# The last feed-forward of a two-layer block on one core: first-half products made and stored beside the second half's routing

## The chip, the core and the metric

One core of one Trainium2 chip runs the whole program as a single launch. The metric is the device time in microseconds; three runs of the kernel before gave a median of 1976.43 us (1968.13 to 1978.0). The core has TensorE (PE; its weight loads are PEld), VectorE (DVE), ScalarE (ACT), GpSimd (POOL) and SyncE (SP). ACT and SP can each issue DMAs on a queue of their own; both queues are served by the same 16 DMA engines.

## The reference

The input is 16 sequences of 256 tokens of 256 numbers. Two attention layers and two feed-forward layers are applied with residual sums. The change touches only the last feed-forward:

```
grouped = x.reshape(b, s // 32, 32, d)                       # 128 groups n of 32 tokens t
logits  = einsum('bntd,des->bntes', grouped, Wc) + bc + tie  # 32 x 4 = 128 experts (e, s)
perm    = (logits == max over t of logits)                   # each expert takes one token of each group
permuted = einsum('bntd,bntes->bnesd', grouped, perm)
inner   = relu(einsum('bnesd,esdf->bnesf', permuted, W1) + b1)   # 256 -> 32
result_permuted = einsum('bnesf,esdf->bnesd', inner, W2) + b2    # 32 -> 256
result  = einsum('bnesd,bntes->bntd', result_permuted, perm)
```

So result_permuted holds 128 groups x 128 experts x 256 float32 numbers, 16 MB, and it does not fit on the core beside the rest. The kernel writes it to HBM (`rp_scratch`, called `rpd`, laid out group, expert, number) and reads it back in another order.

## The kernel before

All five engines run a hand-written program whose order is fixed by semaphores. The last feed-forward begins in the last slots of the attention loop and has two parts.

**Routing, in 20 steps** (`pe_step`, `dve_step`, `act_step`, `pool_step`, n = 0 to 19). A batch b holds 256 tokens, 8 groups. In step n, PE transposes the choice of batch n-2 (L1511), computes the logits of batch n-1 (L1519), transposes the tokens of batch n (L1527) and gathers the chosen tokens of batch n-3 (L1545) into four PSUM banks called `GATHER` (3, 4, 5, 7). ACT copies three of these banks and DVE the fourth into the tile `PX` (L1720, L1633). `PX` has room for 64 groups, so it is filled twice: "halves" 0 and 1. The gather of the next batch waits until these copies are done, since it uses the same four banks. In step 11 (`UP_AT`) PE multiplies half 0 with all of W1 (`pe_up`, L1571, four calls of 32 experts, each with its own 1-MB load of W1), and DVE writes the result with bias and relu into `INT` (`dve_up`). Then routing goes on for batches 9 to 15, into the same `PX`.

**The tail.** `pe_up` for half 1, then 16 calls of `down(q2)`: the second product of 8 experts for all 128 groups, 8 matmuls with 128 groups as output rows into one set of four PSUM banks; DVE and ACT copy two banks each into a 1-MB buffer `RP` (L1703, L1732), and SP stores it (L1779): 128 rows of 8 KB, one per group. The number of `RP` buffers is two for the first four calls and four after them. When all 16 stores have landed, SP reads the 16 MB back (L1787), 8 groups at a time, with experts as partitions, in 1-KB pieces, into six buffers `R2`; PE applies the transpose of the choice (`back`, L1605 and L1608), DVE adds the residual (L1710) and ACT issues the output (L1736), 256 KB for each batch.

SP issues all loads of W1 and W2: six loads of W1 (`first`, L1757) as their buffers come free, two of W2 (`second`, L1761) when the last gather is done, two of W1, then two more of W2 among the stores. In total W1 is read twice (8 MB) and W2 once (4 MB).

The store before is one line. Its destination has 128 rows outermost, as has its source:

```
e.dma_start(rpd[:, 8 * q2:8 * q2 + 8, :], RP[out_at(q2)][:, :, :, :].rearrange("p q r d -> p (q r) d"))
```

Of the kernel before, what the change touches and what calls it, by code (L numbers as in the profile page):

```python
# [56 lines left out]
def build(nc, A, OUT):  # L57
# [1121 lines left out]
    d_ys = [sem(f"d_ys{i}") for i in range(2)]  # L1179
# [109 lines left out]
    def dve_ffn(e, w):  # L1289
# [120 lines left out]
    d_vl = [sem(f"d_vl{i}") for i in range(2)]  # L1410
# [46 lines left out]
    WF2P = [Arena(nc, x3_at)("WF2P0", [128, 8, 256], fp32)]  # L1457
# [3 lines left out]
    WF2P.append(Arena(nc, q1_at)("WF2P1", [128, 8, 256], fp32))  # L1461
    WF1P = [mem_t(f"WF1P{i}", [128, 2, 32, 32], fp32) for i in range(2)]
# [12 lines left out]
    R2 = [mem_t(f"R2{i}", [128, 8, 256], fp32) for i in range(NR)]  # L1475
# [3 lines left out]
    wt_sent, kl_sent = 16, 16 * 32  # L1479
    d_r2 = [sem(f"d_r2{i}") for i in range(NR)]  # L1480
# [10 lines left out]
    def down_set(q2):  # L1491
        return q2 % 2 if q2 >= 4 else 0

    def out_at(q2):
        return q2 % 2 if q2 < 4 else 2 + q2 % 4

    def out_of(q2):

        return q2 - 2 if q2 in (2, 3) else q2 - 4 if q2 >= 8 else None

    def taken_of(q2):

        return q2 if q2 <= 4 else q2 - 1

    def pe_step(e, w, n):
# [25 lines left out]
        def gather(b):  # L1531
# [4 lines left out]
            w.wait_ge(s_in, 7 if b == 8 else 0)  # L1536
            w.wait_ge(a1.s_tv, 2 * U)
# [20 lines left out]
        if n == UP_AT:  # L1558
            for j in range(4):
                pe_up(e, w, 0, j)  # L1560
        if is_batch(n - 3):
            gather(n - 3)

    def pe_up(e, w, hf, j):
        w.wait_ge(d_kl_wf1[j % 2], kl_sent + 16 * (2 * hf + j // 2 + 1))
        w.wait_ge(s_px, 24 * (hf + 1))
        w.wait_ge(s_py, 8 * (hf + 1))
        for q in range(8):
            for cc in range(2):
# [4 lines left out]

    def pe_tail(e, w):
        def down(q2):
            w.wait_ge(d_wt_wf2[q2 // 4 % 2], wt_sent + 16 * (q2 // 8 + 1))
            w.wait_ge(s_in, 8 + 2 * (q2 // 4) + 2)
            w.wait_ge(s_rb, 32)
            w.wait_ge(s_x3e, 16)  # L1580
            w.wait_ge(s_pm, 48)
            w.wait_ge(s_pb, 16)
            w.wait_ge(s_e0, taken_of(q2))
            w.wait_ge(s_e1, taken_of(q2))
            w.wait_ge(s_in, 16 if q2 >= 4 else 0)
            for q in (2 * q2, 2 * q2 + 1):
                for r in range(4):
                    rows = slice(32 * r, 32 * r + 32)
                    m = e.matmul(PS[DOWN[down_set(q2)][r]][:, q % 2 * 256:q % 2 * 256 + 256], INT[rows, q, :],
                                 WF2P[q // 8 % 2][rows, q % 8, :], start=True, stop=True)  # L1590
            m.then_inc(s_fm, 1)

# [96 lines left out]
    def rp_free(w, q2):  # L1689
        if q2 >= 4:  # L1690
            w.wait_ge(s_u3, 8)
        p = out_of(q2)
        if p is not None:
            w.wait_ge(d_ks_rp[p % 4], ks_sent + 16 * (p // 4 + 1))

    def dve_tail(e, w):
        dve_up(e, w, 1, 0)
        dve_up(e, w, 1, 1)
        for q2 in range(16):
            w.wait_ge(s_fm, q2 + 1)  # L1700
            rp_free(w, q2)
            for r in range(2):
# [606 lines left out]
```

## Time and profile before

| | |
|---|---|
| median of 3 runs | 1976.43 us |
| the profiled execution: its own time | 1972.35 us |
| its span, first to last instruction | 1970.5 us |
| PE, DVE, ACT, POOL busy | 90%, 72%, 57%, 39% |
| mean granted TensorE clock | 0.957 |
| last feed-forward, from the first `pe_up` to the end (1799.6 to 1970.5 us) | 170.9 us |

The page gives averages of the whole span; in its 40 slices the last seven (each 49.3 us) differ from the rest. Views used: the stretches ("windows": busy time of each engine, granted clock, DMA busy share of the 16 DMA engines, GB/s), the chain of work that ended last, the instructions in order of time, the DMA view (packets, sizes, issue to landing), and the rows of single source lines.

### The profile page before, as it was taken

The page shows a single profiled execution, that of the slowest core. Times are in us where ns is not written, and L with a number is a line of the kernel's source. Part 1 is how long each engine was busy: PE and PEld are TensorE (multiplying, and loading weights), DVE is VectorE, ACT ScalarE, POOL GpSimd, SP SyncE. Part 2 cuts the span into 40 slices and gives each one's busy share as a digit, 9 for nine tenths or more (in the row PEclk, how much of TensorE's full clock was granted, in tenths as well). Part 3 has the DMA queues.
Part 4 walks back from the last instruction along what each step waited for, and adds up shares of the span by engine and source line. Part 5 has one row for each costly group of instructions (what it writes and reads, how often), then busy time and mean ns, then how long its engine had stood idle before and what let it go on. Part 6 is the DMA issues. An engine that isn't in the chain of part 4 may idle for free.

```text
span 1970.5 us, 41315 instructions
## 1 busy us (share of the span) xinstructions
PE 1774.4 (90%) x15920; PEld 1480.3 (75%) x15920; DVE 1416.2 (72%) x2887; ACT 1129.7 (57%) x2812; POOL 776.3 (39%) x1160
## 2 busy tenths in 40 slices
PE   4788889889899999999999978999999999997647
PEld 3565656656889899999999967887888888876522
DVE  4667777774271488888898658999999999766521
ACT  1344555553334677777777557777777777743310
POOL 1202221101001133333333168788888887644100
PEclk8789999999999999999999989999999999999867
DMA  6444433332577666666776752222222221112599
GB/s 195 108 76 87 86 81 82 80 85 92 202 280 252 226 231 246 247 239 234 248 248 222 245 180 65 65 86 66 66 87 66 65 87 55 53 47 88 202 368 328
DMA packets 134116, 298.70 MB, mean 152 GB/s; under 512 B 13152, under 2 KB 77408, under 8 KB 118688
## 3 DMA queue, kind: packets, MB, share of 16 engines
q1 hardware_dynamic: 111520, 186.18, 30.5%
q0 software_dynamic: 18048, 105.69, 15.6%
q10 hardware_dynamic: 4352, 4.20, 0.6%
q8 instruction: 126, 2.06, 0.4%
q14 instruction: 70, 0.57, 0.1%
HBM read 207.93 MB, written 87.82 MB: 150 GB/s over the span
## 4 chain that ended last, share of the span: by engine, by line
PE 72%; DVE 13%; DMA 7%; issue 3%; POOL 2%; ACT 2%; SPq 1%; DVEq 0%; POOLq 0%; ACTq 0%
PE ps L1232 11%; PE ps L1218 11%; PE ps L1814 5%; PE ps L362 5%; PE ps L214 4%; PE ps L1845 4%; PE ps L1834 4%; PE ps L1800 4%; PE ps L368 3%; PE ps L464 2%; DVE NM L601 2%; DMA R<-rp_scratch 2%; DVE NM L180 2%; PE ps L453 2%; PE ps L441 2%
## 5 line engine op out<-in xcount | busy, mean ns | idle before, releaser
L191 ACT ACTIVATE P<-ps,NM 128x256 f32<-128x256 f32 x512 | 235.8, 474 | 157.3 <-DVE NM L180 157.2
L204 POOL TENSOR_TENSOR P<-P,RS 128x1024 f32<-128x1024 f32 x128 | 246.0, 1922 | 84.9 <-DVE RS L198 84.5
L601 DVE TENSOR_REDUCE NM<-ps 128x2 f32<-128x512 f32 x256 | 164.7, 686 | 111.7 <-PE ps L441 111.6
L1218 PE MATMUL ps<-XRP,W1P 128*128 128x256 f32 x1872 | 226.5, 281 | 4.1 <-DVE W1P L1301 4.1
L712 ACT ACTIVATE PT<-ps 128x512 f32<-128x512 f32 x256 | 138.7, 593 | 150.1 <-PE ps L453 147.9
L1218 PEld LDWEIGHTS ps<-XRP,W1P 128*128 128x128 f32 x1872 | 219.8, 190 | 4.4 <-DVE W1P L1301 4.4
L1232 PE MATMUL ps<-W2P,HP 128*128 128x256 f32 x1872 | 221.3, 277 | 0.0
L1232 PEld LDWEIGHTS ps<-W2P,HP 128*128 128x128 f32 x1872 | 217.7, 188 | 0.0
L138 POOL TENSOR_TENSOR LTMP<-RSTD 128x2 f32<-128x2 f32 (+1 forms) x156 | 32.3, 207 | 351.1 <-DVE RSTD L131 342.8
L180 DVE TENSOR_REDUCE NM<-ps 128x2 f32<-128x512 f32 x256 | 164.2, 683 | 4.9 <-PE ps L1800 3.0
L1261 ACT ACTIVATE HF<-ps,WE 128x256 f32<-128x256 f32 x312 | 129.0, 465 | 43.8 <-PE ps L1218 43.8
L1152 POOL DMA_INDIRECT WE<-in_we,WIX x39 | 44.4, 1139 | 276.2 <-DVE W1P L1301 209.9
L1800 PEld LDWEIGHTS ps<-K,Q 64*128 64x128 f32 x1536 | 101.7, 190 | 59.8 <-issue 47.0
L221 ACT ACTIVATE PT<-ps 128x512 f32<-128x512 f32 x256 | 140.3, 614 | 1.2 <-PE ps L214 1.2
L1814 PE MATMUL ps<-PT,V 128*64 128x256 f32 x1024 | 138.8, 392 | 1.6 <-DVE OT L1935 1.6
L1800 PE MATMUL ps<-K,Q 64*128 64x256 f32 x1536 | 128.3, 300 | 11.0 <-DVE Q L1927 6.2
L214 PE MATMUL ps<-CST,P 128*128 128x128 f32 x1024 | 133.5, 273 | 1.9 <-ACT PT L221 1.5
L1252 ACT ACTIVATE W2P<-WE 128x512 fp32r<-128x512 f32 x156 | 97.3, 623 | 53.1 <-PE ps L1232 53.1
L1148 POOL DMA_INDIRECT XR<-xn_scratch,RIX x78 | 79.0, 1012 | 107.8 <-PE ps L1194 51.0
L1834 PE MATMUL ps<-XNP,W1Q 128*128 128x256 f32 x768 | 111.6, 296 | 9.3 <-POOL XNP L2107 9.3
L214 PEld LDWEIGHTS ps<-CST,P 128*128 128x128 f32 x1024 | 115.1, 141 | 3.4 <-issue 2.5
L1318 DVE TENSOR_TENSOR HP<-HF,HP 128x512 fp32r<-128x512 f32 x156 | 108.0, 693 | 13.0 <-ACT HP L1268 4.0
(220 smaller groups left out, 3832.4 us busy)
## 6 DMA issues: line engine op xcount, KB each, us to landing
KS<-k_scratch SPq DMA_DIRECT2D x64, 256.0 KB, 3.5
V<-v_scratch SPq DMA_DIRECT2D x16, 1024.0 KB
rp_scratch<-RP SPq DMA_DIRECT2D x16, 1024.0 KB
R<-rp_scratch SPq DMA_DIRECT2D x16, 1024.0 KB, 14.0
k_scratch<-KVM SPq DMA_DIRECT2D x54, 256.0 KB
QS<-q_scratch SPq DMA_DIRECT2D x96, 128.0 KB, 4.3
v_scratch<-KVM SPq DMA_DIRECT2D x40, 256.0 KB
ys_scratch<-YS SPq DMA_DIRECT2D x39, 256.0 KB, 8.3
```

What stands on the lines that cost most here:

```text
L180: e.tensor_reduce(self.NM[:, u % 4, 2 * x:2 * x + 2], PS[SB[n % 3]][:, :].rearrange("p (h j) -> p h j", h=2), AX.X, ALU.max, negate=True). ...
L191: i = e.activation(self.P[u % 4][:, c, :], PS[SB[n % 3]][:, y * 256:y * 256 + 256], ACT.Exp, bias=self.NM[:, u % 4, c:c + 1], accum_out=se ...
L204: e.tensor_tensor(p, p, self.RS[:, u % 4, :].unsqueeze(2).to_broadcast([128, 4, 256]), ALU.mult).then_inc(self.s_pn, 1)
L214: i = e.transpose(PS[TB[h]][:, c0:c0 + 128], self.P[u % 4][:, c, jt * 128:jt * 128 + 128], ident)
L221: e.activation(self.PT[u % 4][h][:, :], PS[TB[h]][:, :], ACT.Copy).then_inc(self.s_tv, 1)
L601: e.tensor_reduce(NM0[b % 2][:, :, 8 * h + p], PS[SB[(2 * u + h) % 3]][:, :].rearrange("p (l j) -> p l j", l=2), AX.X, ALU.max, negate=Tru ...
L712: e.activation(PT0[u % 4][h][:, :], PS[TB[h]][:, :], ACT.Exp).then_inc(s_ex0, 1)
L1218: m = e.matmul(PS[p][:, hh * 256:hh * 256 + 256], W1P[i % 2][wi][:, cc * 1024 + hc * 128:cc * 1024 + hc * 128 + 128], XRP[i % 2][xi][:, cc ...
L1232: m = e.matmul(PS[4 + k][:, s * 256:s * 256 + 256], HP[k][hi][:, hc, s * 128:s * 128 + 128], W2P[k][wi][:, hc * 256:hc * 256 + 256], start ...
L1800: m = e.matmul(PS[SB[(2 * u + h) % 3]][:, lt * 256:lt * 256 + 256], Q1[i][64 * h:64 * h + 64, p, lt * 128:lt * 128 + 128], K1[j][64 * h:64 ...
L1814: m = e.matmul(PS[OB][64 * h:64 * h + 64, 0:256], V1[b % 2][:, jt, (2 * p + h) * 64:(2 * p + h) * 64 + 64], a1.PT[u % 4][h][:, jt * 256:jt ...
L1834: m = e.matmul(QB[:, j * 256:j * 256 + 256], W1Q[wi][:, cc, c0:c0 + 128], XNP[b % 2][xi][:, cc, :], start=(cc == 0 and x == 0), stop=(cc = ...
```

## The change

- The second products of half 0 are made in steps 12 to 19, one call of `pe_down(n)` per step ahead of the gather, instead of in the tail. Each call now makes the products of 16 experts for the 64 groups of one half: 16 matmuls of 64 output rows. Experts q with j = 0 go to PSUM rows 0 to 63 and those with j = 1 to rows 64 to 127. There are again 16 calls, 8 for each half, and each fills a 1-MB buffer.
- Calls 0 to 5 use the four `GATHER` banks, since the other banks hold the routing. `pe_down(n)` waits until the last gather was copied out, and the next gather waits until ACT and DVE have copied the products (`s_e0`, `s_e1`). Calls 6 to 9 use the other set.
- The buffer's partition is (j, group), and SP's store has the destination pattern "j p (x d)": 2, then 64 groups, then 8 KB. The source stays 128 partitions of 8 KB. Ten calls use two `RP` buffers; then there are four.
- W2 is read for each half; its last quarter is kept from the first to the second half, so 7 MB instead of 4. The loads of W1 for half 1 all come after step 18. The late loads (four of W1, three of W2) are issued by ACT, the early ones by SP.
- ACT issues the first two of the 16 reads of `rpd` after call 11 (their eight groups each belong to half 0), and SP issues reads 2 to 5 as each of the last four stores has landed. The rest come when all have.
- Some semaphores are used for a second purpose (`d_ys_rp`, `d_vl_rp`); this adds no instruction.

```diff
-    WF2P = [Arena(nc, x3_at)("WF2P0", [128, 8, 256], fp32)]
+    WUP = {"C": Arena(nc, x3_at)("WUPC", [128, 2, 32, 32], fp32)}
+    WDN = {"C": Arena(nc, x3_at)("WDNC", [128, 8, 256], fp32)}
...
-    WF2P.append(Arena(nc, q1_at)("WF2P1", [128, 8, 256], fp32))
-    WF1P = [mem_t(f"WF1P{i}", [128, 2, 32, 32], fp32) for i in range(2)]
+    WDN["D"] = Arena(nc, q1_at)("WDND", [128, 8, 256], fp32)
+    for x in "AB":
+        WDN[x] = Arena(nc, mem_t.at)(f"WDN{x}", [128, 8, 256], fp32)
+        WUP[x] = mem_t(f"WUP{x}", [128, 2, 32, 32], fp32)
...
-    R2 = [mem_t(f"R2{i}", [128, 8, 256], fp32) for i in range(NR)]
+    R2 = [mem_t(f"R2{i}", [128, 8, 256], fp32) for i in (2, 3, 4, 5, 0, 1)]
+    R2 = R2[4:] + R2[:4]
...
+    LATE_STORES = ((d_ys_rp[0], 16 * 20), (d_ys_rp[1], 16 * 19), (d_vl_rp[0], 16 * 8), (d_vl_rp[1], 16 * 8))
...
-    def down_set(q2):
-        return q2 % 2 if q2 >= 4 else 0
-    def out_at(q2):
-        return q2 % 2 if q2 < 4 else 2 + q2 % 4
-    def out_of(q2):
-        return q2 - 2 if q2 in (2, 3) else q2 - 4 if q2 >= 8 else None
-    def taken_of(q2):
-        return q2 if q2 <= 4 else q2 - 1
+    LOADS = {"A": (d_kl_wf1[0], kl_sent), "B": (d_kl_wf1[1], kl_sent), "C": (d_wt_wf2[0], wt_sent), "D": (d_wt_wf2[1], wt_sent)}
+    UP_IN = (("A", 1), ("B", 1), ("A", 2), ("B", 2), ("A", 5), ("C", 1), ("A", 6), ("C", 2))
+    DOWN_IN = (("A", 3), ("B", 3), ("A", 4), ("B", 4), ("D", 1), ("A", 7), ("C", 3), ("B", 4))
+    def loaded(w, at):
+        d, n0 = LOADS[at[0]]
+        w.wait_ge(d, n0 + 16 * at[1])
+    def down_set(n):
+        return 1 if n < 6 else 0 if n < 10 else n % 2
+    def out_at(n):
+        return n % 2 if n < 10 else 2 + n % 4
+    def out_of(n):
+        return n - 2 if 2 <= n < 10 else n - 4 if n >= 14 else None
+    def taken_of(n):
+        return 0 if n == 6 else n if n <= 10 else n - 1
...
+            w.wait_ge(s_e0, min(b - 8, 6))
+            w.wait_ge(s_e1, min(b - 8, 6))
...
+        if n > UP_AT:
+            pe_down(e, w, n - UP_AT - 1)
         if is_batch(n - 3):
             gather(n - 3)
+    def pe_down(e, w, n):
+        at = DOWN_IN[n // 2]
+        hf, t = n // 8, n % 8
+        loaded(w, at)
+        w.wait_ge(s_in, 8 * hf + 2 * (t // 2) + 2)
+        if n < 6:
+            w.wait_ge(s_px, 3 * (n + 9))
+            w.wait_ge(s_py, n + 9)
+        else:
+            w.wait_ge(s_rb, 32)
+            w.wait_ge(s_x3e, 16)
+            w.wait_ge(s_pm, 48)
+            w.wait_ge(s_pb, 16)
+        w.wait_ge(s_e0, taken_of(n))
+        w.wait_ge(s_e1, taken_of(n))
+        w.wait_ge(s_in, 16 if n >= 10 else 0)
+        for k in range(2):
+            for j in range(2):
+                q = 4 * t + 2 * j + k
+                for r in range(4):
+                    rows = slice(32 * r, 32 * r + 32)
+                    m = e.matmul(PS[DOWN[down_set(n)][r]][64 * j:64 * j + 64, k * 256:k * 256 + 256],
+                                 INT[rows, q, hf * 64:hf * 64 + 64], WDN[at[0]][rows, q % 8, :], start=True, stop=True)
+        m.then_inc(s_fm, 1)
...
-        for q2 in range(16):
-            down(q2)
-            if q2 < 2:
-                pe_up(e, w, 1, q2 + 2)
+        for n in range(8, 16):
+            pe_down(e, w, n)
+            if n < 10:
+                pe_up(e, w, 1, n - 6)
...
+        if n > UP_AT:
+            dve_out(e, w, n - UP_AT - 1)
...
+    def landed(w, n):
+        if n < 8:
+            w.wait_ge(d_ks_rp[n % 4], ks_sent + 16 * (n // 4 + 1))
+        else:
+            d, n0 = LATE_STORES[n % 4]
+            w.wait_ge(d, n0 + 16 * (n // 4 - 1))
...
+    def rp_free(w, n):
+        w.wait_ge(s_om, 32)
+        w.wait_ge(s_u3, 8 if n >= 10 else 0)
+        p = out_of(n)
         if p is not None:
-            w.wait_ge(d_ks_rp[p % 4], ks_sent + 16 * (p // 4 + 1))
+            landed(w, p)
...
+    def dve_out(e, w, n):
+        w.wait_ge(s_fm, n + 1)
+        rp_free(w, n)
+        for r in range(2):
+            i = e.tensor_copy(RP[out_at(n)][:, :, r, :], product(n, r))
+        i.then_inc(s_e0, 1)
+    def act_out(e, w, n):
+        w.wait_ge(s_fm, n + 1)
+        rp_free(w, n)
+        for r in range(2, 4):
+            i = e.activation(RP[out_at(n)][:, :, r, :], product(n, r), ACT.Copy)
+        i.then_inc(s_e1, 1)
...
+        if n > UP_AT:
+            act_out(e, w, n - UP_AT - 1)
+        if n == UP_AT + 7:
+            w.wait_ge(s_fm, 6)
+            first(e, 4)
+            w.wait_ge(s_x3p, 32)
+            w.wait_ge(s_x3t, 16)
+            first(e, 5)
+        elif n == UP_AT + 8:
+            w.wait_ge(s_ga, 16)
+            second(e, 4)
     def act_tail(e, w):
-        w.wait_ge(s_om, 32)
-        for q2 in range(16):
-            w.wait_ge(s_fm, q2 + 1)
-            rp_free(w, q2)
-            for r in range(2, 4):
-                i = e.activation(RP[out_at(q2)][:, :, r, :], PS[DOWN[down_set(q2)][r]][:, :].rearrange("p (q d) -> p q d", q=2), ACT.Copy)
-            i.then_inc(s_e1, 1)
+        for j in (6, 7):
+            w.wait_ge(s_u3, j - 1)
+            first(e, j)
+        act_out(e, w, 8)
+        w.wait_ge(s_u3, 7)
+        second(e, 5)
+        act_out(e, w, 9)
+        w.wait_ge(s_u3, 8)
+        second(e, 6)
+        act_out(e, w, 10)
+        act_out(e, w, 11)
+        for n in range(4):
+            landed(w, n + 4)
+        for b in range(2):
+            back_in(e, w, b)
+        for n in range(12, 16):
+            act_out(e, w, n)
...
+    def first(e, j):
+        x = UP_IN[j][0]
+        e.dma_start(WUP[x][:, :, :, :], A["wf1"][:, :, 32 * (j % 4):32 * (j % 4) + 32, :]).then_inc(LOADS[x][0], 16)
+    def second(e, j):
+        x = DOWN_IN[j][0]
+        e.dma_start(WDN[x][:, :, :], A["wf2"][:, 8 * (j % 4):8 * (j % 4) + 8, :]).then_inc(LOADS[x][0], 16)
+    def back_in(e, w, b):
+        w.wait_ge(s_cm2, b - NR + 1)
+        e.dma_start(R2[b % NR][:, :, :], rpd[8 * b:8 * b + 8, :, :].rearrange("n s d -> s n d")).then_inc(d_r2[b % NR], 16)
     def sp_tail(e, w):
-        def first(j):
-            w.wait_ge(s_u3, j - 1)
-            e.dma_start(WF1P[j % 2][:, :, :, :], A["wf1"][:, :, 32 * (j % 4):32 * (j % 4) + 32, :]).then_inc(d_kl_wf1[j % 2], 16)
-        def second(j):
-            w.wait_ge(s_fm, 4 * (j - 1))
-            e.dma_start(WF2P[j % 2][:, :, :], A["wf2"][:, 8 * j:8 * j + 8, :]).then_inc(d_wt_wf2[j % 2], 16)
+        def store(n):
+            hf, t = n // 8, n % 8
+            w.wait_ge(s_e0, n + 1)
+            w.wait_ge(s_e1, n + 1)
+            to = rpd[64 * hf:64 * hf + 64, 16 * t:16 * t + 16, :].rearrange("p (j x) d -> j p (x d)", j=2)
+            e.dma_start(to, RP[out_at(n)][:, :, :, :].rearrange("p k r d -> p (k r d)")).then_inc(LATE_STORES[n % 4][0] if hf else d_ks_rp[n % 4], 16)
...
-        for j in range(6):
-            first(j)
-        w.wait_ge(s_ga, 16)
-        second(0)
-        second(1)
-        first(6)
-        first(7)
-        for q2 in range(16):
-            w.wait_ge(s_e0, q2 + 1)
-            w.wait_ge(s_e1, q2 + 1)
-            e.dma_start(rpd[:, 8 * q2:8 * q2 + 8, :], RP[out_at(q2)][:, :, :, :].rearrange("p q r d -> p (q r) d")).then_inc(d_ks_rp[q2 % 4], 16)
-            if q2 in (3, 7):
-                second(q2 // 4 + 2)
         for j in range(4):
-            w.wait_ge(d_ks_rp[j], ks_sent + 16 * 4)
-        w.wait_ge(s_u3, 8)
-        for b in range(16):
-            w.wait_ge(s_cm2, b - NR + 1)
-            e.dma_start(R2[b % NR][:, :, :], rpd[8 * b:8 * b + 8, :, :].rearrange("n s d -> s n d")).then_inc(d_r2[b % NR], 16)
+            w.wait_ge(s_u3, j - 1)
+            first(e, j)
+        for j in range(2):
+            w.wait_ge(s_u3, j + 3)
+            second(e, j)
+        for n in range(8):
+            store(n)
+            if n in (1, 3):
+                w.wait_ge(s_fm, n + 1)
+                second(e, n // 2 + 2)
+        for n in range(8, 16):
+            store(n)
+        for b in range(2, 6):
+            landed(w, 10 + b)
+            back_in(e, w, b)
...
+        for n in range(8, 12):
+            landed(w, n + 4)
+        for b in range(6, 16):
+            back_in(e, w, b)
```

## Rows read from the trace of the kernel before

**Rows 1.** The page: engines, and DMA in 40 slices of 49.3 us.

```profile
PE 1774.4 (90%) x15920; PEld 1480.3 (75%) x15920; DVE 1416.2 (72%) x2887; ACT 1129.7 (57%) x2812; POOL 776.3 (39%) x1160
...
DMA  6444433332577666666776752222222221112599
GB/s 195 108 76 87 86 81 82 80 85 92 202 280 252 226 231 246 247 239 234 248 248 222 245 180 65 65 86 66 66 87 66 65 87 55 53 47 88 202 368 328
```

**Rows 2.** Stretches: step 11, steps 12 to 19, products and stores, last landing, reads.

```profile
core 0: us, PE busy (x) PEld busy (x) DVE busy (x) ACT busy (x) POOL busy (x), PEclk, DMA share, GB/s
...
1799.60:1815.00 15.40, 9.53 (x516) 8.78 (x516) 5.73 (x13) 0.58 (x1) 0.53 (x1) 0.89 0.53 178
1815.00:1840.40 25.40, 18.16 (x305) 15.13 (x307) 16.03 (x36) 15.27 (x28) 11.59 (x12) 0.90 0.20 67
1840.40:1897.30 56.90, 34.19 (x768) 25.98 (x768) 24.87 (x40) 17.32 (x32) 0.00 (x0) 0.77 0.91 361
1897.30:1905.80 8.50, 0.00 (x0) 0.00 (x0) 0.00 (x0) 0.00 (x0) 0.00 (x0) 0.50 0.70 297
1905.80:1970.50 64.70, 44.09 (x320) 18.38 (x320) 11.00 (x16) 0.00 (x0) 0.00 (x0) 0.73 0.96 325
```

**Rows 3.** The chain of work that ended last, 1838 to 1912 us: start, length, what.

```profile
1871.94 11.24 DMA rp_scratch<-RP
...
1884.59 11.25 DMA rp_scratch<-RP
...
1895.94 1.30 DVE RP L1703 x2
1897.24 0.02 issue
1897.26 8.40 DMA rp_scratch<-RP
```

**Rows 4.** Stretches of saturated stores, and of saturated reads with output.

```profile
1870.00:1900.00 30.00, 12.69 (x136) 8.07 (x128) 12.23 (x20) 10.23 (x20) 0.00 (x0) 0.72 1.01 421
1912.00:1960.00 48.00, 36.72 (x271) 15.35 (x272) 8.93 (x13) 0.00 (x0) 0.00 (x0) 0.75 1.09 368
```

**Rows 5.** In order of time, a routing step: start, length, instruction, [idle before].

```profile
1814.95 1.11 PE L1545 MATMUL ps<-PB,X3P 32*128 32x128 f32 x32 [0.88 <-DVE RL L1684]
...
1818.70 0.66 PE L1527 MATMUL ps<-CST,X 128*128 128x128 f32 x4 [1.40 <-issue]
...
1819.29 1.11 PE L1545 MATMUL ps<-PB,X3P 32*128 32x128 f32 x32
...
1820.46 1.63 ACT L1720 ACTIVATE PX<-ps 128x512 f32<-128x512 f32 x3 [0.46 <-PE ps L1545]
...
1822.19 1.07 PE L1545 MATMUL ps<-PB,X3P 32*128 32x128 f32 x29
```

**Rows 6.** In order of time, one call of down and its copies.

```profile
1848.07 1.15 PE L1589 MATMUL ps<-WF2P,INT 32*128 32x256 f32 x16
...
1849.29 1.29 DVE L1703 COPY RP<-ps 128x512 f32<-128x512 f32 x2
1849.35 1.09 ACT L1732 ACTIVATE RP<-ps 128x512 f32<-128x512 f32 x2 [9.05 <-PE ps L1589]
```

**Rows 7.** DMA view, 68.9 to 71.5 us: four 4-KB transfers of eight 512-byte pieces.

```profile
DMA packets 64, 0.02 MB, mean 6 GB/s; under 512 B 32, under 2 KB 64, under 8 KB 64
```

**Rows 8.** DMA view, 1734 to 1741 us: one transfer of 128 rows of 1 KB, then others.

```profile
DMA packets 156, 0.18 MB, mean 26 GB/s; under 512 B 16, under 2 KB 144, under 8 KB 156
...
B<-in_b SPq DMA_DIRECT2D x1, 128.0 KB, 2.0
```

**Rows 9.** DMA view, 1870 to 1900 us: packets of the saturated stores.

```profile
DMA packets 1729, 12.62 MB, mean 421 GB/s; under 512 B 191, under 2 KB 191, under 8 KB 191
```

**Rows 10.** SP's queue in order of time: issues.

```profile
1838.71 0.81 SPq L1761 DMA_DIRECT2D WF2P<-in_wf  x2
1844.09 4.63 SPq L1757 DMA_DIRECT2D WF1P<-in_wf  x2
...
1877.29 20.28 SPq L1779 DMA_DIRECT2D rp_scratch<-RP  x8
1905.80 8.87 SPq L1787 DMA_DIRECT2D R<-rp_scratch  x5
```

**Rows 11.** Stretches around a fall of the granted clock in the routing.

```profile
1776.00:1788.00 12.00, 7.21 (x119) 5.93 (x118) 11.52 (x34) 5.68 (x11) 8.02 (x25) 0.99 0.01 2
1788.00:1791.00 3.00, 3.00 (x14) 2.20 (x13) 2.07 (x6) 1.07 (x2) 2.52 (x6) 0.50 0.00 0
1819.30:1833.70 14.40, 12.17 (x199) 10.10 (x199) 11.46 (x27) 10.49 (x19) 9.34 (x10) 1.00 0.02 5
```

More of the change, by code:

```diff
@@ L1178, in build @@
     assert mem.at <= base1 + FFN_AT
-    d_ys = [sem(f"d_ys{i}") for i in range(2)]
+    d_ys_rp = [sem(f"d_ys_rp{i}") for i in range(2)]
     s_ft, s_xrp, s_um, s_ge, s_hp = sem("xrT"), sem("xrp"), sem("upmm"), sem("gelu"), sem("hp")
@@ L1409, in build @@
     d_gy = [sem(f"d_gy{i}") for i in range(4)]
-    d_vl = [sem(f"d_vl{i}") for i in range(2)]
+    d_vl_rp = [sem(f"d_vl_rp{i}") for i in range(2)]
     s_ca, s_wh, s_wl, s_tanh = sem("moe_add"), sem("wqo_hi"), sem("wqo_lo"), sem("tanh")
@@ L1575, in pe_tail @@
     def pe_tail(e, w):
[L1576 to L1591, printed above, removed]
         def back(b):
@@ L1698, in dve_tail @@
         dve_up(e, w, 1, 1)
-        for q2 in range(16):
-            w.wait_ge(s_fm, q2 + 1)
-            rp_free(w, q2)
-            for r in range(2):
-                i = e.tensor_copy(RP[out_at(q2)][:, :, r, :], PS[DOWN[down_set(q2)][r]][:, :].rearrange("p (q d) -> p q d", q=2))
-            i.then_inc(s_e0, 1)
-            if q2 < 2:
-                dve_up(e, w, 1, q2 + 2)
+        for n in range(8, 16):
+            dve_out(e, w, n)
+            if n < 10:
+                dve_up(e, w, 1, n - 6)
         for b in range(16):
@@ L1768, in sp_tail @@
         e.dma_start(B2[:, :], A["b2_1"]).then_inc(d_c1, 16)
-        for j in range(6):
-            first(j)
-        w.wait_ge(s_ga, 16)
-        second(0)
-        second(1)
-        first(6)
-        first(7)
-        for q2 in range(16):
-            w.wait_ge(s_e0, q2 + 1)
-            w.wait_ge(s_e1, q2 + 1)
-            e.dma_start(rpd[:, 8 * q2:8 * q2 + 8, :], RP[out_at(q2)][:, :, :, :].rearrange("p q r d -> p (q r) d")).then_inc(d_ks_rp[q2 % 4], 16)
-            if q2 in (3, 7):
-                second(q2 // 4 + 2)
-        for j in range(4):
-            w.wait_ge(d_ks_rp[j], ks_sent + 16 * 4)
-        w.wait_ge(s_u3, 8)
-        for b in range(16):
-            w.wait_ge(s_cm2, b - NR + 1)
-            e.dma_start(R2[b % NR][:, :, :], rpd[8 * b:8 * b + 8, :, :].rearrange("n s d -> s n d")).then_inc(d_r2[b % NR], 16)
+        for j in range(4):
+            w.wait_ge(s_u3, j - 1)
[8 more added lines that the diff above has]
+                second(e, n // 2 + 2)
+        for n in range(8, 16):
+            store(n)
[6 more added lines that the diff above has]
+            back_in(e, w, b)
         for j in range(4):
@@ L2060, in act_l1 @@
             late_out(e, w, t)
-        w.wait_ge(d_ys[0], 16 * 20)
-        w.wait_ge(d_ys[1], 16 * 19)
+        w.wait_ge(d_ys_rp[0], 16 * 20)
+        w.wait_ge(d_ys_rp[1], 16 * 19)
         w.wait_ge(s_ye, NTF)
@@ L2109, in pool_l1 @@
         w.wait_ge(s_ft, NTF)
-        w.wait_ge(d_ys[0], 16 * 20)
-        w.wait_ge(d_ys[1], 16 * 19)
+        w.wait_ge(d_ys_rp[0], 16 * 20)
+        w.wait_ge(d_ys_rp[1], 16 * 19)
         for j in range(4):
```

20 lines of the change are left out of this document (9 added, 11 removed).

## The prediction, made before the changed kernel was seen to run

> **What bounds the kernel now.** I read the page first. PE is busy for 90% of the span, but the DMA rows show that the last slices are another kind of work: 202 to 368 GB/s, against 47 to 88 before them [rows 1]. The stretches of the last feed-forward then show who works [rows 2]. While half 1 is routed (1815 to 1840 us) the DMA engines are at 0.20 of their time and PE at 18.2 of 25.4 us. After 1840.4 it is the reverse: DMA share 0.91, then 0.70, then 0.96. The chain of waits says the same: from 1871.9 us it consists of stores to `rp_scratch`, 11.2 us at a time, with a 1.3-us copy between them, until the last store has landed (8.4 us after the last copy) [rows 3]. In saturated stretches the 16 engines move 421 GB/s of stores and 368 GB/s of reads with outputs, both at a share of 1.01 or more [rows 4]. So the tail is bound by the DMA engines, and PE's granted clock there (0.72 to 0.77) costs little. The idea of the change follows from these rows: 8 MB of stores, 20 us at 421 GB/s, move into a stretch in which DMA idles. What it is worth hangs on whether a store in its new form still runs at 421 GB/s.
>
> **Part 1: the routing steps become longer.** A step is now 2.90 us: gather (started 1819.29), copy to `PX` by ACT (1820.46, 1.63 us), next gather at 1822.19 [rows 5]. In steps 12 to 17 a call and its copies come in between, since they use the gather's banks: 1.22 us from the call to DVE's copy (1848.07 to 1849.29), 1.29 us of copy, and 0.2 us until the waiting PE goes on [rows 6]. That is 2.7 us on the path, six times: 16 us. ACT's two copies (1.09 us) lie beside DVE's. The call has 16 matmuls of 64 output rows where the row has 8 of 128; if these overlap as before it stays 1.15 us, and if not at all it is 2.3 us, 7 us more in six steps. I take 1.15, because the work per bank is the same. A longer step leaves PE emptier, and before the clock's fall to 1.2 GHz (share 0.50) at 1788 us PE was busy for 60% of 12 us, against 85% in the steps of now at full clock [rows 11]. A step would have about 4.1 of 5.6 us, 73%, so a fall or two of 3 us is to be expected: 1 to 5 us. Behind the waiting PE are queued only the next gather, behind ACT's wait its copies and loads.
>
> **Part 2: the loads.** W1's four loads of half 1 come after call 5's products are copied, where two of them had been there early and two were issued at 1844 to 1848 us [rows 10]; W2 is read in 7 pieces instead of 4. At 421 GB/s [rows 4] a 1-MB load holds all engines for 2.5 us. ACT issues seven of them, at some 0.5 us each, ahead of copies that aren't urgent then.
>
> **Part 3: the form of the stores.** This decides. Before, both sides of a store have 128 rows outermost. Now the destination has 2, then 64, then 8 KB. What number of engines does a transfer use? The DMA view shows it. Four transfers of eight 512-byte pieces have 32 data packets and 32 packets below 512 bytes [rows 7], 8 small ones for each transfer. A transfer of 128 rows of 1 KB has 128 data packets and 16 small ones [rows 8]. The small packets are no data (the pieces alone make up the 4 KB), so I read them as one signal of each engine that took part: 8 engines where the outermost count is 8, 16 where it is 128. If the outermost count sets it, a new store runs on 2 engines, one for each j. All rows of before fit this reading, but none has a small outermost count with many rows inside, so it isn't proved by them.
>
> The Trainium skill states that case: "DMA: Bandwidth & Descriptors", section "Why a DMA increments its semaphore by 16 and not by 1", says that the transfer is split along the slowest dimension other than 1 of each side, over the largest number of engines up to 16 that divides both. The trace agrees for 8 and for 128; by it the store here would run on 2. It adds that these are always the lowest-numbered ones; no row shows it.
>
> The price: 421 GB/s over 16 engines is 26.3 GB/s for each [rows 4], and the stores' packets are 8 KB there already (1538 of 1729 packets are not under 8 KB; the others are below 512 bytes) [rows 9], so an engine can't gain from larger ones. 1 MB over two engines takes 1048576 / 52600 = 19.9 us instead of 2.5. All 16 stores come from one queue. If each takes the same pair, these two engines are one lane through which everything passes, the loads' and reads' sixteenth parts too.
>
> **The sum of the forecast.** Call 0 starts where gather 9 did, at 1819.3; with 1.2 and 1.3 us [rows 6] its store is issued at 1821.9 and flows from some 1823.0. Then the pair has to do: 16 stores of 19.9 = 318.4 us; nine 1-MB loads (two early ones of W2 behind stores in SP's queue, seven late ones) of 2.5 = 22.5; the two reads ahead of the rest, 1 MB at 368 GB/s = 2.85 each, 5.7. Together 346.6 us, to 2169.6. Gaps: call n may be copied when store n-2 has landed, so that one more store is always under way while 1.3 us of copy and the issue go on; and between the landing of store 5, which frees call 7 and ACT's load of the next W2, and the end of store 7 lie some 45 us, for a chain of about 30 (one load, `pe_up`, another load, a call). I take no gap; 1 us at each store would be 16. Afterwards the reads: from the first issue at 1905.80 to the end they took 64.7 us [rows 2, 10]. Two with their outputs are done (2 x 1.31 MB at 368 GB/s = 7.1 us), and the start of 2.0 us falls away, since reads 2 to 4 are queued behind the last stores: 55.6 us. End: 2225.2 instead of 1970.5, so 254.7 us more. Set on the profiled execution's own 1972.35 this is 2227.1. That execution lies 4.1 us under the median of the runs, 1976.43; on the median it is **2231 us**. All of part 1 is hidden in it: with 20-us stores the steps wait for buffers, not for PE, and the clock doesn't matter.
>
> The forecast's own range: down by 36 us if the pair moves a store in 17.7 us (29.6 GB/s for each; nothing shows over 26.3), up by 16 for a gap of 1 us at each store and 18 for loads that hold the pair longer: 2195 to 2265.
>
> **Rivals.**
> 1. *Sixteen engines carry the store.* The count follows the number of rows, 8 in one case and 128 in the other, and rows 7 and 8 fit this as well. It decides from eight engines on: a store then takes 5.0 us and fits in a step of 5.6. Then the late loads begin 15.6 us later than at 1838.7 [rows 10]; six stores less after that point are 14.9 us, one load more 2.5; of the idle DMA time (9% of 56.9, 30% of 8.5 and the reads' start [rows 2]) some 8 us are filled, since reads 0 to 5 run beside the last stores. 15.6 + 2.5 - 14.9 - 8 = -4.8 us, and with 3 for the clock 1975 us, from 1960 (full clock, no idle) to 1990 (calls of 2.3 us, clock low). This ends not slower.
> 2. *Two engines for each store, but another pair each time.* With two buffers two stores are under way: four pairs of stores of half 0 take 4 x 24 us (19.9 + landing, copy, issue), stores 8 and 9 another 24, and with four buffers two rounds from there. The last lands near 1979 and the end is at 2032, 62 us more: 2038. The sixteen small packets of rows 8 say nothing of it; that eight-piece transfers would rotate isn't seen either.
>
> **Chances.** Forecast 0.86, rival 1 0.10, rival 2 0.04. Within rival 1 the time is faster by over 0.5% (9.9 us, about what a measurement of this kernel can tell from no change) in 0.03, within it in 0.05, slower in 0.02. Together: faster 0.03, same 0.05, slower 0.92. The range is the forecast's own: it holds nearly all of its 0.86, which leaves out under 2 in 10.
>
> **What the changed profile would show.** Right: from 1823 us on a DMA share near 2/16, 0.13, and some 53 GB/s, for over 300 us; DVE and ACT idle before their copies of products, released by stores, some 20 us apart; PE at about 1 us in 20 in steps 14 to 19; the reads at 368 GB/s only in the last 50 us. A store's small packets would be 2. Part 1 wouldn't be seen in the time, but the first gap, call 0 to gather 9, would be 2.7 us. Wrong: a DMA share near 1 during the stores in the tail (rival 1), or 0.25 with landings 10 us apart (rival 2). A lane of over 27 GB/s for each engine would shorten the forecast in proportion.

## The result, and the profile after

The changed kernel takes 2222.94 us, the median of 4 runs (2218.54 to 2229.72); the kernel before, on the same chip, 1975.33 us (4 runs). The ratio is 1.1253, with a 95% interval from 1.1224 to 1.1281: 12.5% slower. The span of the profiled execution is 2220.7 us, 250.2 us longer than before.

The page, the rows that answer to [rows 1] (its 40 slices are now 55.5 us long):

```profile
PE 1790.3 (81%) x16176; PEld 1488.8 (67%) x16176; DVE 1416.2 (64%) x2887; ACT 1129.5 (51%) x2812; POOL 776.2 (35%) x1160
...
PEclk8899999899999999999999999999999995555557
DMA  6533344326776666667662122222221122232128
GB/s 189 108 77 78 77 87 87 77 98 224 279 245 229 238 239 236 248 250 242 233 214 81 63 82 64 81 66 78 67 73 51 41 87 86 87 120 103 62 79 307
```

Every engine has as many busy microseconds as before, within 1%: work was not added, time was. The slices that held 202 to 368 GB/s are gone but for the last one. The stretches of the tail show what took their place (columns as in [rows 2]):

```profile
1822.00:1843.00 21.00, 8.28 (x124) 6.14 (x120) 6.98 (x15) 5.85 (x11) 3.77 (x4) 0.74 0.26 97
1843.00:1930.00 87.00, 23.96 (x338) 17.15 (x338) 13.82 (x26) 13.69 (x26) 5.63 (x6) 0.54 0.17 68
1930.00:1960.00 30.00, 7.45 (x264) 6.80 (x256) 3.43 (x6) 1.08 (x2) 0.00 (x0) 0.50 0.48 188
1960.00:2100.00 140.00, 26.64 (x552) 16.64 (x552) 13.72 (x22) 8.68 (x16) 0.00 (x0) 0.57 0.22 85
2100.00:2168.00 68.00, 0.00 (x0) 0.00 (x0) 0.00 (x0) 0.00 (x0) 0.00 (x0) 0.50 0.22 81
...
2175.00:2220.70 45.70, 32.90 (x246) 13.58 (x240) 8.93 (x13) 0.00 (x0) 0.00 (x0) 0.78 0.90 309
```

From 1843 to 2168 us no engine is busy for even a third of the time, and the DMA engines are at 0.17 to 0.22 of theirs, but for 30 us in which late loads pass (1930 to 1960, 0.48). In the last 68 us of it nothing computes at all (2100 to 2168). Only the last 46 us look like the reads of before. DVE's copies of products in order of time (its other instructions are left out) say what was waited for:

```profile
1826.48 1.29 DVE L1740 COPY RP<-ps 128x512 f32<-128x512 f32 x2 [0.35 <-PE ps L1603]
1842.68 1.29 DVE L1740 COPY RP<-ps 128x512 f32<-128x512 f32 x2 [11.02 <-DMA rp_scratch<-RP]
1863.13 1.29 DVE L1740 COPY RP<-ps 128x512 f32<-128x512 f32 x2 [13.32 <-DMA rp_scratch<-RP]
1885.19 1.29 DVE L1740 COPY RP<-ps 128x512 f32<-128x512 f32 x2 [14.93 <-DMA rp_scratch<-RP]
1904.77 1.29 DVE L1740 COPY RP<-ps 128x512 f32<-128x512 f32 x2 [15.13 <-DMA rp_scratch<-RP]
1926.81 1.29 DVE L1740 COPY RP<-ps 128x512 f32<-128x512 f32 x2 [17.93 <-DMA rp_scratch<-RP]
```

Calls 0 and 1 are copied as soon as PE has made them, 7 us apart. From call 2 to call 9 each copy is released by the landing of a store, and from 1842.68 us on the starts shown are 19.6 to 22.1 us apart. (Calls 10 to 13 have buffers of their own and wait for PE; calls 14 and 15 wait for stores again.) Two stores are under way at any time, so if these had different engines, the landings would come about twice as often. The wait view sums it up: ACT waits 213.8 us and DVE 209.7 us for the landing of stores.

The DMA view of 2040 to 2060 us lies inside one long wait:

```profile
DMA packets 209, 1.06 MB, mean 53 GB/s; under 512 B 4, under 2 KB 90, under 8 KB 90
```

53 GB/s are 26.5 for each of two engines. Most of it is stores; 86 of the packets have 1 KB and belong to ACT's two early reads. From 2056 to 2094 us there are only 8-KB packets of stores, and two stores land (the copies at 2067.66 and 2087.24 us are released by them):

```profile
DMA packets 252, 2.03 MB, mean 53 GB/s; under 512 B 4, under 2 KB 4, under 8 KB 4
...
q1 hardware_dynamic: 252, 2.03, 12.6%
```

12.6% of 16 engines are two engines, and four small packets for two stores are two for each. This is the plainest row.

### The profile page after: what moved, and what is told of

Same layout as the page of the kernel before. It is cut to its first block, busy times and chain, and to the rows that moved or that the text cites. A ratio compares the mean times of both kernels' runs of the same rounds, so it can differ in the third digit from the quotient of the medians.

```text
span 2220.7 us, 41828 instructions
## 1 busy us (share of the span) xinstructions
PE 1790.3 (81%) x16176; PEld 1488.8 (67%) x16176; DVE 1416.2 (64%) x2887; ACT 1129.5 (51%) x2812; POOL 776.2 (35%) x1160
## 4 chain that ended last, share of the span: by engine, by line
PE 63%; DMA 12%; DVE 11%; SPq 4%; another core or an unknown queue 3%; issue 3%; POOL 2%; ACT 1%; DVEq 0%; POOLq 0%; ACTq 0%
PE ps L1232 10%; PE ps L1218 10%; DMA rp_scratch<-RP 8%; PE ps L1897 4%; PE ps L362 4%; PE ps L214 4%; PE ps L1928 4%; PE ps L1917 3%; PE ps L1883 3%; PE ps L368 3%; PE ps L464 2%; SPq L1835 2%; DVE NM L601 2%; DMA R<-rp_scratch 2%
## 5 line engine op out<-in xcount | busy, mean ns | idle before, releaser
L1740 DVE COPY RP<-ps 128x512 f32<-128x512 f32 x32 | 20.6, 686 | 218.0 <-DMA rp_scratch<-RP 209.7
L1632 PE MATMUL ps<-B2S,PMT 128*128 128x256 f32 x64 | 20.9, 417 | 156.8 <-DMA R<-rp_scratch 83.6
L1632 PEld LDWEIGHTS ps<-B2S,PMT 128*128 128x128 f32 x64 | 12.9, 253 | 176.7 <-DMA R<-rp_scratch 92.7
L1747 ACT ACTIVATE RP<-ps 128x512 f32<-128x512 f32 x32 | 17.4, 595 | 223.2 <-DMA rp_scratch<-RP 213.8
```

## The experiments

"Before" means the kernel before run in the same session: 1976.19 us (19 runs) for the first four, 1974.91 (23 runs) for the next four, 1975.19 (13 runs) for the last two.

### Is it the outermost count of 2? Two transfers of 64 rows

```diff
-            to = rpd[64 * hf:64 * hf + 64, 16 * t:16 * t + 16, :].rearrange("p (j x) d -> j p (x d)", j=2)
-            e.dma_start(to, RP[out_at(n)][:, :, :, :].rearrange("p k r d -> p (k r d)")).then_inc(..., 16)
+            for j in range(2):
+                to = rpd[64 * hf:64 * hf + 64, 16 * t + 8 * j:16 * t + 8 * j + 8, :].rearrange("p x d -> p (x d)")
+                e.dma_start(to, RP[out_at(n)][64 * j:64 * j + 64, :, :, :].rearrange("p k r d -> p (k r d)")).then_inc(..., 16)
```

The same bytes go from the same places to the same places. All else is as in the changed kernel; the waits on landings count 32 for 16.

> The changed kernel with one alteration: each 1-MB store is issued as two transfers of 64 rows of 8 KB, one for each j, so that the outermost count of both sides is 64 and not 2. Bytes, piece size, order and buffers stay. Theory 1 (a transfer's engines are set by its outermost count; a store in the changed form runs on 2 of 16, 19.9 us): the stores go back to about 421 GB/s and 2.5 us for 1 MB, and the time falls from 2223 to about 1975 us (1960 to 1990), as worked out for sixteen engines in the prediction. Theory 2 (what costs is the place of the stores and calls in the routing steps, or the late loads on ACT's queue): the time stays over 2100 us.

Measured: 1976.22 us (10 runs), ratio to before 0.9998 [0.9972, 1.0023]. All of the 247 us is gone. The stretches now read:

```profile
1815.00:1860.00 45.00, 32.83 (x544) 23.10 (x533) 25.44 (x50) 21.27 (x39) 11.29 (x12) 0.77 0.78 227
1860.00:1920.00 60.00, 27.84 (x832) 19.26 (x829) 17.40 (x29) 11.26 (x21) 0.00 (x0) 0.67 0.96 340
1920.00:1960.00 40.00, 25.01 (x220) 10.87 (x220) 7.56 (x11) 0.00 (x0) 0.00 (x0) 0.89 1.08 368
```

The form of the destination pattern is the whole loss. The routing with its calls, the load order and the early reads together cost and bring nothing that these medians can tell.

### The same loss put into the kernel before: cuts of 68 + 60 and 64 + 64 rows

```diff
-            e.dma_start(rpd[:, 8 * q2:8 * q2 + 8, :], RP[out_at(q2)][:, :, :, :].rearrange("p q r d -> p (q r) d")).then_inc(d_ks_rp[q2 % 4], 16)
+            for a, z in ((0, 68), (68, 128)):
+                e.dma_start(rpd[a:z, 8 * q2:8 * q2 + 8, :], RP[out_at(q2)][a:z, :, :, :].rearrange("p q r d -> p (q r) d")).then_inc(d_ks_rp[q2 % 4], 16)
```

> The kernel before with each 1-MB store cut into two transfers, of 68 and of 60 rows. Theory 1 in the form that the number of engines is the largest one up to 16 that divides the outermost count: 68 rows run on 4 engines (17 rows each, 17 x 0.31 = 5.3 us), 60 rows on 15 (4 rows each, 1.2 us); where both fall on the same engines, a store takes 6.5 us there instead of 2.5: 16 x 4.0 = 64 us more, less some 8 us that DMA idles now, so about 2031 us (2015 to 2045). Theory 3 (small outermost counts limit the engines, but any count from 16 on gives all): no change, 1975 us within 10.

> The kernel before with each store cut into two transfers of 64 rows: the control for the number of transfers. Both theories: within 5 us of the kernel before (1975), since 64 rows divide over 16 engines and SP has time for 16 more issues of 0.32 us. A time over 1985 would mean that cutting a store costs by itself, and this would have to come off the other runs.

Measured for 68 + 60 (one run): 2030.36 us. DVE in order of time shows the period:

```profile
1918.98 1.29 DVE L1703 COPY RP<-ps 128x512 f32<-128x512 f32 x2 [7.59 <-DMA rp_scratch<-RP]
1925.42 1.29 DVE L1703 COPY RP<-ps 128x512 f32<-128x512 f32 x2 [5.15 <-DMA rp_scratch<-RP]
1931.87 1.29 DVE L1703 COPY RP<-ps 128x512 f32<-128x512 f32 x2 [5.16 <-DMA rp_scratch<-RP]
1938.29 1.29 DVE L1703 COPY RP<-ps 128x512 f32<-128x512 f32 x2 [5.14 <-DMA rp_scratch<-RP]
```

6.42 to 6.45 us between copies, where 6.5 was worked out from 4 engines for 68 rows and 15 for 60 with the lower engines shared. The small packets, one for each engine that takes part, can be counted too. Three stores land between 1920 and 1938 us:

```profile
DMA packets 425, 3.02 MB, mean 168 GB/s; under 512 B 57, under 2 KB 57, under 8 KB 57
```

57 are 19 for each store, 4 + 15. It is no matter of fewer rows or more transfers: 64 + 64 has both and takes 1984.09 us (10 runs), ratio 1.0046 [1.0016, 1.0076]. That is 8 to 9 us more than before, above the 5 allowed; where they come from stayed open until the cuts of the reads, below.

### Outermost 2 in another form, and for half of the stores

> The changed kernel with each store cut into two transfers that both keep the outermost count 2: each carries 4-KB pieces (half of the experts of a row) of all 128 partitions. Theory 1, with the same two engines for every transfer: 64 packets of 4 KB on each of two engines, 0.16 us each, 10.2 us for half a store, 20.4 for a store against 19.9: 2230 us, within 15. If the pair changed from one transfer to the next, two halves would run side by side and a store take about 10 us: near 2070 us. If the cost came from the 8-KB pieces or from one transfer's size of 1 MB, the time would fall clearly under 2200.

The edit cuts each store by the pieces, not by the rows: two transfers of 512 KB, each still "j p (y d)" with 2 outermost. Measured (one run): 2222.67 us. The DMA view of 2040 to 2060 us:

```profile
DMA packets 262, 1.06 MB, mean 53 GB/s; under 512 B 4, under 2 KB 4, under 8 KB 262
```

Twice as many transfers with 4-KB packets move the same 53 GB/s: two transfers in flight share the two engines. This run has the number and the size of the transfers of the first experiment and the outermost count of the changed kernel, and it is as slow as the latter. The time lies within 0.3 us of the changed kernel's, but that flatters the form: this execution came to its first copy of products at 1814.04 us, 5.5 us earlier than the changed kernel's (1819.54), and ended at the same time. Its copies are 19.9 us apart (1880.60, 1900.49) where those are 19.6, so 4-KB packets cost some 0.3 us for each store, where 0.5 was expected.

> The changed kernel with its own two-outermost stores for half 0 (8 stores) and stores cut into two of 64 rows for half 1. A dose of half: by the sum of the prediction with 8 stores of 19.9 us in place of 16 (8 x 17.4 = 139 us less), 2223 - 139 = 2084 us (2070 to 2095). If what costs were not a fixed 17.4 us for each store but a state that the first such store brings about (a blocked queue), the time would stay near 2223; if the stores under the routing steps were covered, it would be near 1976.

Here half 0's stores keep the changed form and half 1's are split as in the first experiment. Measured (one run): 2090.82 us, within the expected range. 8 slow stores cost 116 us and 16 cost 247, about 15 us for each (14.5 for each of the eight of half 0, and 16.5 for each of the other eight). A store is slow by 17.1 us (19.6 for 2.5), but the first of them lie beside the routing, in time in which the DMA engines stood at 0.20 before [rows 2]. That this is the difference of 2 to 3 us is argued, not isolated.

### What the rest of the change is worth with fast stores

```diff
-            to = rpd[64 * hf:64 * hf + 64, 16 * t:16 * t + 16, :].rearrange("p (j x) d -> j p (x d)", j=2)
+            to = rpd.rearrange("n (h e) d -> (n h) e d", h=2)[128 * hf:128 * hf + 128, 8 * t:8 * t + 8, :]
```

> The changed kernel with each store as one transfer of 128 rows of 8 KB at a uniform distance of 64 KB. Bytes, pieces, order and waits stay; the rows of a half are put in the other order within this half's 8 MB, so the read-back hands experts and groups of a half to each other wrongly and that part of the output is left wrong. It prices the restructured stage with a store that is neither on two engines nor cut in two. The control with cut stores was 8 to 9 us over the kernel before, and the restructured stage with cut stores equal to it. If cutting costs the same in both, this one comes out 8 us under the kernel before: 1968 (1962 to 1974). If cutting cost something only where the stores are the bound, it stays at 1976 within 4.

Measured: 1975.55 us (12 runs), ratio 1.0000 [0.9981, 1.002], where 1968 was expected. The diff shows the destination; the source is as before, and one part of the output isn't the reference's. The forecast value took the 8 us that the cut into 64 + 64 rows costs the kernel before and subtracted them here. The other case that the expectation names came out: the medians show no gain over the cut stores. Whether there is none is another matter, see "The stage alone" below.

> The first of these kernels (rows of a half in the other order, that part of the output left wrong) without the early reads: all 16 reads are issued by SP after the last store has landed, as in the kernel before. By the working of the prediction, the two reads ahead (7.1 us with their outputs, of which the reads are 5.7) and the start of 2 us are what early reads give when DMA engines would idle otherwise, but they also take their bandwidth from the last stores: between 3 and 8 us slower than the kernel with early reads. If the whole gain lay in the stores' move, no difference.

Measured: 1976.5 us (12 runs), ratio 1.0019 [1.0, 1.0038]. The medians give 1 us for the early reads, but the interval of this ratio reaches 7 us, so 3 to 8 isn't excluded. The stretches of the one with early reads:

```profile
1815.00:1860.00 45.00, 32.21 (x613) 22.77 (x609) 25.03 (x50) 18.89 (x35) 11.28 (x12) 0.80 0.61 228
1860.00:1920.00 60.00, 31.16 (x884) 21.70 (x868) 18.92 (x31) 13.58 (x26) 0.00 (x0) 0.67 0.95 355
1920.00:1960.00 40.00, 31.64 (x231) 13.58 (x232) 7.56 (x11) 0.00 (x0) 0.00 (x0) 0.71 1.09 369
```

From 1860 us on the DMA engines are nearly full. Without the early reads their share is 0.87 to 0.96 from 1860 to 1920 us, and 1.09 after; from 1900 to 1920 us they move 301 GB/s where they move 402 with them. So there is some idle time to fill, a few us and no more; where there is none, a read put earlier only takes the place of a load or a store that comes later.

### A correct order with 128 uniform rows, and why it is slow

> As the one before, but computing the reference: j is now the upper half of the experts (q = 16 j + 2 t + k), so that the 128 rows of a store are uniformly spaced and still the right ones; W2 comes in two 4-KB pieces for each partition instead of one of 8 KB, W1's quarters in the order 0, 2, 1, 3, and each read of 1 MB is cut into two of 64 partitions. If the reads' pieces (1 KB, 1024 of them) bound them and not the number of transfers, the same time as the one before plus one bias step (1 us) and under 2 us for the loads: 1970 (1963 to 1978). If cut reads cost as cut stores did (16 times 0.5 us), 1977.

Measured: 1996.14 us (6 runs), ratio 1.0115 [1.0085, 1.0144]: 26 us above the one value (1970) and 19 above the other (1977). The stretch of its reads:

```profile
1920.00:1990.00 70.00, 46.47 (x280) 18.50 (x280) 9.63 (x14) 0.00 (x0) 0.00 (x0) 0.59 1.11 254
```

A DMA share of 1.11, as full as before's 1.09 [rows 4], and yet 254 GB/s for 368. What differs is that a read now consists of two transfers of 64 partitions. Two cuts of the reads of the kernel before tell that apart from the number of transfers:

```diff
-            e.dma_start(R2[b % NR][:, :, :], rpd[8 * b:8 * b + 8, :, :].rearrange("n s d -> s n d")).then_inc(d_r2[b % NR], 16)
+            for a in (0, 64):
+                e.dma_start(R2[b % NR][a:a + 64, :, :], rpd[8 * b:8 * b + 8, a:a + 64, :].rearrange("n s d -> s n d")).then_inc(d_r2[b % NR], 16)
```

```diff
+            for a in (0, 4):
+                e.dma_start(R2[b % NR][:, a:a + 4, :], rpd[8 * b + a:8 * b + a + 4, :, :].rearrange("n s d -> s n d")).then_inc(d_r2[b % NR], 16)
```

> The kernel before, each of the 16 reads cut into two transfers of 64 partitions. It tests why the version with correct order and 128 uniform rows took 21 us more than the one with the wrong order. There DMA share in the stretch of the reads was 1.12 to 1.14, as full as in the others (1.09), but it moved only 236 to 263 GB/s where they moved 368 to 371. Theory: a transfer that writes 64 partitions moves each packet more slowly, whatever kernel it is in. From 1905.8 to the end 16 MB (16.8 million bytes) are read; at 370 GB/s that is 45 us, at 255 GB/s 66 us: expected 21 us later than before, 1996 us (1990 to 2000), with about 255 GB/s at a share over 1.1. Rival: it lay in the order in which the other version's rows lie in memory, or in its loads in 4-KB pieces: then this one takes what before takes, 1976 (up to 1984 for the doubled number of transfers, as with the stores cut in 64 + 64), at 360 GB/s or more.

> The kernel before, each of the 16 reads cut into two transfers as well, but each of them over all 128 partitions with 4 of the 8 pieces of every partition. Number of transfers and bytes of each as in the cut by partitions. Theory (64 partitions are what is slow): 1976 us, at most 1984, GB/s of the reads 360 to 370. Rival (twice as many transfers, half as large, are what is slow): the same time as the version cut by partitions, 1990 to 2000.

Measured: by partitions 2001.65 us (4 runs), ratio 1.0132 [1.0084, 1.018], 26 us more where 21 were expected, a little outside the 1990 to 2000; by pieces 1977.42 us (10 runs), ratio 1.002 [1.0001, 1.004]. The reads cut by partitions, the stretch and then the packets of 1925 to 1955 us:

```profile
1920.00:1990.00 70.00, 45.30 (x280) 18.23 (x280) 8.94 (x13) 0.00 (x0) 0.00 (x0) 0.56 1.12 257
```

```profile
GB/s 193 227 382 363 212 363 378 213 210 223 199 198 201 228 197 352 381 239 272 400 298 198 206 231 199 202 223 203 244 378 350 210 317 384 273 214 221 199 212 201
DMA packets 7884, 7.80 MB, mean 260 GB/s; under 512 B 287, under 2 KB 7883, under 8 KB 7883
```

Cut by pieces, the stretch from 1920 to 1960 us:

```profile
1920.00:1960.00 40.00, 25.85 (x212) 11.01 (x212) 7.56 (x11) 0.00 (x0) 0.00 (x0) 0.87 1.09 371
```

The number of transfers is not what costs; 64 partitions are. Why they do is open. With 16 engines at a share of 1.12 for 30 us, 7884 packets took 68 ns each. In the kernel before, 11109 packets of the same size took 47 ns over the same 30 us at 1.09. The 40 slices show two levels, near 200 and near 380 GB/s. The higher one would be the time in which transfers of both halves are under way at once, but no row names the halves, so this is a reading and not shown.

The 8 to 9 us of the cut into 64 + 64 rows fit it. The profiled execution with cut stores reaches its first store 6 us later, so equal work has to be compared, from the issue of the first store to the last copy. Before (first line) this takes 45 us, with the cut 52, at the same share:

```profile
1850.60:1896.00 45.40, 25.87 (x460) 18.33 (x448) 20.16 (x33) 15.21 (x29) 0.00 (x0) 0.77 0.92 368
1856.50:1909.00 52.50, 25.78 (x494) 18.80 (x483) 20.15 (x34) 15.28 (x29) 0.00 (x0) 0.77 0.92 318
```

The last 13 us with the cut, with stores of both halves queued, run at 414 GB/s and a share of 1.01, which fits the two levels. The changed kernel shows it as well: from 1815 to 1860 us it moves 227 GB/s at a share of 0.78 with cut stores, and 228 at 0.61 with stores of 128 rows.

**The stage alone.** The runs of one kernel differ by up to 20 us (1964 to 1984 for the kernel before), and much of that arises ahead of the stage: its first instruction, the first `pe_up`, starts between 1793.9 and 1803.7 us in the profiled executions, though the code ahead of it is the same. Counted from there to the end of the span, one execution of each:

| kernel | stage, us |
|---|---|
| before | 170.9 |
| before, reads cut by pieces | 171.2 |
| before, stores cut 64 + 64 | 181.2 |
| before, reads cut by partitions | 197.7 |
| before, stores cut 68 + 60 | 230.3 |
| changed | 421.5 |
| changed, stores cut into 4-KB pieces | 427.0 |
| changed, stores of half 1 cut 64 + 64 | 289.9 |
| changed, all stores cut 64 + 64 | 175.1 |
| changed, 128 rows | 170.5 |
| changed, 128 rows, late reads | 175.8 |
| changed, 128 rows, correct order, reads cut | 197.4 |

The cut of the reads costs 27 us in both kernels, which leaves next to nothing for the order in memory or for W2's 4-KB pieces. The restructured stage with the best stores equals the stage before, 170.5 against 170.9 us. The early reads give 5.3 us here, inside the 3 to 8 expected, and 128 rows 4.6 against 64 + 64. How far the stage itself varies from run to run isn't known, so these two stay open between the 1 us of the medians and the 5 us here.

## Why the prediction was right

2231 us (2195 to 2265) was forecast, 2222.94 measured. The main step held: an outermost count of 2 gives two engines. It stood on two indirect rows [rows 7, 8]. The first experiment showed it by removing that count alone, the cut into 68 and 60 rows by another count, and half of the stores by its dose. By the rule in "DMA: Bandwidth & Descriptors" of the Trainium skill, section "Why a DMA increments its semaphore by 16 and not by 1" (the largest number up to 16 that divides both sides), 68 rows run on 4 engines and 60 on 15; the 6.4-us period and the 19 small packets for each store agree. The prediction's own sign is there too: two small packets for each store of the changed kernel, in the row of 2056 to 2094 us above.

Step by step:

- **Start.** Call 0 was expected at 1819.3 and its store issued at 1821.9. The call came at 1818.38 and SP issued at 1820.85, 1 us earlier. The gap between call 0 and the next gather is 2.6 us (1818.38 to 1820.93), where 2.7 was forecast.
- **19.9 us for a store, 26.3 GB/s for each engine.** The copies stand 19.6 us apart where no load is in between (1885.19 and 1904.77, 2067.66 and 2087.24). The term was under 2% too long, 5 us over 16 stores.
- **Loads share the lane.** Where they do, the copies are 20.5 to 27.0 us apart; one load makes 22.06 of 19.58, 2.5 us as priced. No gap was taken: by the trace's packet records at least two packets are under way from 1822 to 2167 us but for 0.1 us. The last store was to land by 2169.6 and landed by 2166.9.
- **The reads afterwards.** 55.6 us were expected. From 2166.9 to the end of the span it is 53.8. The chain of waits, from the last issues of SP to the end:

```profile
2104.18 19.35 SPq L1843
2123.59 19.20 SPq L1835
2142.84 19.23 SPq L1835
...
2166.88 2.94 SPq L1835
2169.86 12.48 DMA R<-rp_scratch
...
2217.38 0.69 DVE XO L1760
```

- **The sum** was 254.7 us over before in the span; it is 250.2. The start gives back 1.0 us, the time of the pair 1.7 and the reads 1.8. The rest of the 8 us between 2231 and 2222.94 isn't the mechanism's: the forecast was set 4.1 us over its profiled execution, since the median before lay so far over it; the changed kernel's median lies 0.4 over its own. So how near the two numbers lie is luck to some 4 us.
- **The longer routing steps are hidden.** Right in this kernel: PE waits 59.9 us for DVE's copies of products ahead of six gathers, and the clock of 0.50 to 0.57 from 1843 to 2168 us costs nothing that shows. PE was to be busy for about 1 us in 20; it is 24.0 of 87.0 us from 1843 to 1930, since a step holds the routing's own matmuls too. Nothing in the sum rests on that. The steps' price could be measured with fast stores only. In the first experiment a step takes 5.5 us at full clock (gathers at 1822.56 and 1828.04), where 5.6 was worked out, and 6.3 to 7.0 in the four steps after it, in which the granted clock is lower (0.66 from 1840 to 1860 us). That is some 5 us over five steps, the upper end of the 1 to 5 allowed for the clock; the sum of rival 1 took 3.
- **Rival 1** gave 1975 us for sixteen engines: 1976.22 and 1975.55 measured, in the middle of its 1960 to 1990. Its condition was false in the changed kernel; where the experiments made it true, its sum came out, including that the stores put beside the routing bring nothing. With 64-row stores the first late load comes at 1858.8 instead of 1838.7, 20 us later (15.6 forecast, 18.6 with its 3 for the clock), and this takes back what the six early stores give. Its 8 us of filled idle time weren't measured apart.
- **Rival 2**, rotating pairs, is excluded by landings 20 us apart with two stores under way, and by the run with two half transfers, which it would have put near 2070. Its own 2038 isn't fully worked out: 1823 and five times 24 us give 1943, two more rounds of 19.9 end near 1983 and not 1979, some 4 us later. Which two engines they are isn't seen.

What missed lay in the expectations of the experiments: the cost of half-partition transfers (8 us for the stores, 27 us for the reads), and the gain of 128 rows over the kernel before (8 us expected, none measured). The gain of the early reads (3 to 8 us expected) isn't settled.

## What to carry to other kernels

Before a DMA's pattern is changed, read its outermost count on both sides and keep it at a number like the 64 and 128 here, which 16 divides; 2 and 68 were slow. One store of 1 MB with 2 outermost took 19.6 us for 2.5, with the same bytes and the same 8-KB pieces. If the data only fits such a pattern, cut the transfer in two along the outermost count; cuts into 64 partitions cost the kernel before 0.5% (stores) and 1.3% (reads), and the changed kernel with cut stores was no slower than before by its median. Reads cut inside the partitions took 1.002 times as long [1.0001, 1.004]. And where a tail is full of DMA from end to end, work moved ahead of it pays only if the loads that it pushes back are not waited for: here 8 MB of stores moved forward were worth 0. A difference of a few us in such a stage is better read from the stage's own start than from whole times, which vary by more ahead of it.

## What was not expected of the hardware

- **Issuing can block.** An issue of a store took 0.32 us before, with the DMA engines full, and 0.5 to 0.6 us in the changed kernel while no more than three stores were queued. The issue of a fourth (at 2007.89 us) took 36 us, those behind it 19 to 20 us each, 19.35 for the last store and 19.20 for the read after it. The issues of two loads behind stores took 10.3 and 17.2 us. What stands behind in SP's queue stands still, a read whose data had landed too: store 12, for which it waits, landed at 2107.8 us. The rows come from windows that hold one issue each, the first from the kernel before; the row that merges the issues of twelve stores, 236.86 us from 1886.67 us on, is half waiting for their data:

```profile
1894.81 0.32 SPq L1779 DMA_DIRECT2D rp_scratch<-RP  x1
1952.69 0.49 SPq L1843 DMA_DIRECT2D rp_scratch<-RP  x1
...
2123.59 19.20 SPq L1835 DMA_DIRECT2D R<-rp_scratch  x1
```

- **A full share is not full speed.** Transfers of 64 partitions showed a share of 1.12 at 257 GB/s, those of 128 partitions 1.09 at 371 GB/s. The share counts the time of packets, not their bytes; both columns must be read.
- **Packets of 4 KB and of 8 KB** both move about 53 GB/s over two engines; a store takes 19.9 us in the one form and 19.6 in the other.
